# One decoder layer on one core: contiguous scratch runs, loads behind them, a shared heads bank, layer norm applied by ScalarE

## The chip, the cores and the metric

The kernel runs on 1 core of a Trainium2 chip. The metric is the device time in microseconds of one execution; a kernel's time is the median of its runs.

## The reference

Four sequences of 256 rows with 128 features pass three blocks, each with a residual and a layer norm. The context has 512 rows per sequence.

```python
x = _layernorm(x + attn(x))               # causal, 16 heads of 8, low-rank W_dq, W_uq, W_dkv, W_uk, W_uv, W_o
x = _layernorm(x + xattn(x, ctx_1024))    # keys: the 512 context rows, then x itself (causal there)
x = _layernorm(x + ffn(x))                # per feature m of 64: relu(s_m * W1 + b1) . W2, 16 inner
# in both attentions, per head:
dots = einsum(q, k) / sqrt(8); attn = softmax(dots); out = einsum(attn, v)
```

## The kernel before

**Units and steps.** A unit is one attention of one sequence: units 0 to 3 are self attention, 4 to 7 cross attention. Each has four groups of four heads, so there are 32 steps, `t` = 0 to 31, 16 of each kind. A step has three kinds of work: **S**, scores with queries on the partitions, of which VectorE takes the maximum over the keys (L1036, L869, L871); **T**, scores with keys on the partitions, whose exponential ScalarE writes into `probs` (L774); and **pv**, the product with the values (L1086). Between S and T the maxima of a step are split into three bf16 parts by GpSimd (L709 to L715), transposed (`shift`, L1097), copied by ScalarE (L801) and sent by DMA into three rows under the queries (`rows`, `send_rows`, L593), where ones under the keys meet them. So the exponential needs no bias. A self step has 4 S tiles and 4 T tiles, a cross step 12 and 12.

**Split operands.** Queries and keys are made in float32 (`qk u` for unit u, `m b` for the keys of context b) and split into three bf16 parts: ScalarE copies the high part (L789), VectorE subtracts (L886), and the middle and low parts are made by GpSimd, or by VectorE for `low_on_dve` (L601). They lie in a ring `spl` of SPL tiles. A **put** (L627) writes them to scratch in DRAM with each part as often as the products need it, six slots in all; a **take** (L646) reads them back so that 48 partitions hold six slots of eight features of one head pair. Scratch holds the features in their order, so a take has 384 runs of 1 KB per half. All puts and takes are issued by SyncE, as are the rows of cross attention; the rows of self attention go by ScalarE's queue. `ones_under` must have filled the tile before its take.

**Heads, norms and the rest.** pv adds into one half bank, `heads`; after each step ScalarE copies it to `headsT` (`drain`, L782), and the next step's pv waits for that (L1075). After four drains `norm` (L1099) transposes with eight matmuls, VectorE divides (L914, L917), and `ln1` adds x and takes moments (L899, L847); GpSimd makes `rstd` (L739, L742) and VectorE applies it (`apply`, L901). `x1T`, `qk u+4` and `v2` follow for cross attention; `yT`, `wo`, `x2T`, `s`, `hid`, `g`, `mo` after it. `v1`, `vm` and `v2` are the values.

**What sets the order.** `schedule()` (L157) plans all stages in one list with costs per engine; every engine walks that list in order, and TensorE never overtakes. `LATE` (L69) names the step before which the operands of later units are not made. Where the plan sees a gap, TensorE gets `warm` matmuls (L958). The start: DMA of `w64` and `wa`, 28 warm matmuls, six folding matmuls (L953), then qk 0, qk 1, v1 0, qk 2, v1 1. SyncE loads the context, x and the biases behind the puts of unit 0 (L643 to L645).

```python
                    if i == 0:
                        sp.dma_start(ctxT_sb[:, :], ctxT).then_inc(ctxT_in, 16)
                        sp.dma_start(x_sb[:, :, :], x_rows.rearrange("(n p) c -> p n c", p=P)).then_inc(x_in, 16)
```

## Time and profile before

| | us |
|---|---|
| Median of 3 runs | 290.76 (288.23 to 294.63) |
| The profiled execution | 293.45 |
| Its span, first to last instruction | 291.7 |
| TensorE busy | 241.0 (83%) |
| VectorE busy | 194.3 (67%) |
| ScalarE busy | 159.8 (55%) |
| GpSimd busy | 99.8 (34%) |

The profiled execution is 1.75 us longer than its span, which is time around the first and last instruction, and 2.7 us longer than the median. Durations in the profile are of this one execution. Matmuls are pipelined and their ends are modelled, so a busy TensorE is not one at its peak. "issue" as a releaser is time in which an engine waited for nothing that the profile shows; PEclk is the clock granted to TensorE, as a share of 2.4 GHz.

### The profile page before, as it was taken

How to read it: one execution, taken by the hardware profiler on the slowest of the kernel's cores; microseconds unless marked ns; L12 is line 12 of the kernel's file. 1: busy time of each engine (PE TensorE's matmuls, PEld its weight loads, DVE VectorE, ACT ScalarE, POOL GpSimd, SP SyncE). 2: the span in 40 equal slices, each digit the busy share in tenths (PEclk: the TensorE clock that was granted, in tenths of full speed). 3: DMA queues.
4: the chain of work that ended last, by engine and by line, in shares of the span. 5: the costliest groups of instructions: out<-in, count | busy, mean ns of one | idle time of the engine just before them, and what ended most of it. 6: DMA issues, size and time to landing. Idle time of an engine off the chain costs nothing.

```text
span 291.7 us, 13772 instructions
## 1 busy us (share of the span) xinstructions
PE 241.0 (83%) x5973; PEld 144.2 (49%) x5973; DVE 194.3 (67%) x429; ACT 159.8 (55%) x367; POOL 99.8 (34%) x250
## 2 busy tenths in 40 slices
PE   8920478689845699999999499999999999999882
PEld 5710336456533446756555156454654465544651
DVE  0830395785232578797999277999889997852652
ACT  1400024455523257676788255988688858879330
POOL 8650074635321142334372101522225212531131
PEclk9985595999977799999999669999999999999998
DMA  4169995101897017353639600000000000000000
GB/s 138 64 202 299 243 205 141 24 8 42 248 186 174 12 57 169 107 117 102 124 106 224 115 3 3 5 5 5 5 3 5 5 5 5 3 5 21 21 18 18
DMA packets 22716, 23.66 MB, mean 81 GB/s; under 512 B 1472, under 2 KB 20224, under 8 KB 22528
## 3 DMA queue, kind: packets, MB, share of 16 engines
q1 hardware_dynamic: 22224, 22.55, 31.7%
q8 instruction: 47, 0.77, 1.2%
q10 hardware_dynamic: 432, 0.23, 0.3%
q14 instruction: 13, 0.11, 0.1%
HBM read 12.62 MB, written 9.96 MB: 77 GB/s over the span
## 4 chain that ended last, share of the span: by engine, by line
PE 42%; DVE 19%; DMA 14%; SPq 9%; issue 7%; ACT 3%; POOL 3%; ACTq 2%; POOLq 0%; DVEq 0%
PE psum L1011 13%; PE psum L1086 10%; DVE pm L869 9%; DMA qk<-shift_rows 6%; DMA qk<-scr_qk 5%; DVE pm L871 4%; PE psum L1106 4%; PE psum L1018 3%; PE psum L958 3%; ACTq L599 2%; ACT probs L774 2%; DMA scr_m<-spl 2%; SPq L635 1%; PE psum L1173 1%; SPq L634 1%
## 5 line engine op out<-in xcount | busy, mean ns | idle before, releaser
L774 ACT ACTIVATE probs<-psum 128x512 f32<-128x512 f32 (+1 forms) x256 | 120.6, 554 | 41.6 <-PE psum L1011 20.9
L1011 PE MATMUL psum<-qk 51*32 51x128 bf16 (+3 forms) x2048 | 63.2, 266 | 31.7 <-DMA qk<-scr_qk 20.9
L871 DVE TENSOR_REDUCE pm<-psum 128x3 f32<-128x384 f32 x128 | 63.5, 550 | 36.6 <-PE psum L1018 36.5
L869 DVE TENSOR_REDUCE pm<-psum 128x1 f32<-128x512 f32 x128 | 79.1, 681 | 7.0 <-PE psum L1011 7.0
L1086 PE MATMUL psum<-probs,v 128*9 128x256 f32 (+1 forms) x1024 | 66.1, 368 | 3.5 <-issue 2.8
L1011 PEld LDWEIGHTS psum<-qk 48*32 48x32 bf16 (+1 forms) x2048 | 35.2, 96 | 56.1 <-DMA qk<-scr_qk 21.5
L1011 PE MATMUL psum<-qk,km 51*32 51x256 bf16 x1024 | 37.9, 278 | 2.8 <-DMA qk<-shift_rows 2.5
L724 POOL TENSOR_SCALAR_AFFINE_SELECT probs<-probs 128x512 f32<-128x512 f32 x32 | 20.3, 640 | 57.0 <-ACT probs L774 56.7
L1086 PEld LDWEIGHTS psum<-probs,v 128*9 128x9 f32 x1024 | 23.2, 91 | 26.0 <-issue 13.8
L1011 PE MATMUL psum<-km,qk 48*32 48x512 bf16 x512 | 35.6, 394 | 0.2
L1018 PE MATMUL psum<-neg,unit_b 64*32 64x256 bf16 x512 | 31.5, 305 | 0.0
L709 POOL CAST max_s<-maxima 128x8 bf16<-128x8 f32 x32 | 6.1, 191 | 66.4 <-DVE maxima L876 66.4
L789 ACT ACTIVATE spl<-psum 128x512 bf16<-128x512 f32 x12 | 7.2, 597 | 33.9 <-PE psum L1135 26.9
L1011 PEld LDWEIGHTS psum<-qk,km 51*32 51x32 bf16 x1024 | 15.3, 92 | 18.9 <-issue 5.5
L801 ACT ACTIVATE shift_rows<-psum 12x256 bf16<-12x256 f32 x32 | 11.5, 366 | 18.5 <-PE psum L1097 17.4
L1018 PE MATMUL psum<-negT,unit_b 64*32 64x256 bf16 x256 | 16.5, 299 | 0.0
L958 PE MATMUL psum<-warm 128*128 128x256 bf16 x97 | 15.2, 306 | 1.2 <-DVE warm L826 1.2
L1106 PEld LDWEIGHTS psum<-wa_sb,headsT 128*128 128x128 f32 x128 | 15.2, 194 | 1.7 <-DVE pm L871 0.9
L1106 PE MATMUL psum<-wa_sb,headsT 128*128 128x36 f32 x128 | 15.6, 279 | 0.1
L1011 PEld LDWEIGHTS psum<-km,qk 48*32 48x32 bf16 x512 | 12.0, 92 | 7.2 <-DVE pm L869 2.0
L1018 PEld LDWEIGHTS psum<-neg,unit_b 64*32 64x32 bf16 x512 | 14.1, 101 | 0.0
L782 ACT ACTIVATE headsT<-psum 128x256 f32<-128x256 f32 x32 | 12.0, 374 | 3.3 <-issue 2.3
(98 smaller groups left out, 263.7 us busy)
## 6 DMA issues: line engine op xcount, KB each, us to landing
qk<-scr_qk SPq DMA_DIRECT2D x16, 384.0 KB, 6.4
scr_qk<-spl SPq DMA_DIRECT2D x8, 384.0 KB, 5.1
scr_qk<-spl SPq DMA_DIRECT2D x24, 128.0 KB, 5.1
km<-scr_m SPq DMA_DIRECT2D x8, 384.0 KB, 6.8
scr_m<-spl SPq DMA_DIRECT2D x4, 384.0 KB, 3.1
ctxT_sb<-ctxT SPq DMA_DIRECT2D x1, 1024.0 KB, 5.7
scr_m<-spl SPq DMA_DIRECT2D x4, 256.0 KB, 3.5
wb_sb<-wb SPq DMA_DIRECT2D x1, 642.0 KB, 4.5
```

Source lines behind the costliest of these rows:

```text
L724: nc.gpsimd.affine_select(out=tile, in_=tile, compare_op=ALU.is_ge, fill=0.0, base=0, pattern=[[0, 2], [0, 2], [1, P]], channel_multiplier ...
L774: nc.scalar.activation(probs[:, ring % PRING, r, 0:cols], bank_of(s)[:, 0:cols], ACT.Exp, scale=SCALE).then_inc(exp_done, 1)
L782: nc.scalar.activation(headsT[:, t % (2 * NG), :], heads[:, 0:T], ACT.Copy).then_inc(drained, 1)
L789: nc.scalar.activation(parts_of(s)[0], m, ACT.Copy).then_inc(split_high, 1)
L801: last = nc.scalar.activation(shift_rows[:, t % ROWBUFS, :], m[0:PARTS * HG, 0:T], ACT.Copy, scale=-1.0)
L869: nc.vector.tensor_reduce(pm[:, place, 1 + 4 * qt:2 + 4 * qt], m, axis=AX.X, op=ALU.max).then_inc(reduced, 1)
L871: nc.vector.tensor_reduce(pm[:, place, 2:5], own_blocks(m), axis=AX.X, op=ALU.max).then_inc(reduced, 1)
L958: nc.tensor.matmul(m[:, 0:T], warm[:, 0:P], warm[:, 0:T], start=True, stop=True)
L1011: last = nc.tensor.matmul(o[STRIP * c:STRIP * (c + 1)], lhs[:, STRIP * c:STRIP * (c + 1)], rhs, start=start, stop=stop, skip_group_check=True)
L1018: last = nc.tensor.matmul(o[STRIP * c:STRIP * (c + 1)], half(unit_b, r, HALF), half(rows, r, HALF)[:, c, :, :], start=False, stop=True, sk ...
L1086: last = nc.tensor.matmul(heads[STRIP * j:STRIP * j + HS + 1, q0:T], v, weights, start=(k == 0), stop=(k == len(key_tiles(t)) - 1))
L1106: last = nc.tensor.matmul(m[:, n * cols:(n + 1) * cols], headsT[:, at, qt * P:(qt + 1) * P], used_rows, start=True, stop=True)
```

## The change

- Scratch is laid out as [half, slot, feature, ...] and the features of a half are ordered by dimension, then pair (the weights are permuted to match), so that each of the 48 partitions of a take reads one run of 8 KB. Puts and takes are made by halves of 64 partitions: 8 DMAs for a qk, 6 for an m. For qk 0 to 2 one half goes by ScalarE's queue.
- The loads of `wb`, x, biases and context stand behind the takes of units 1, 2 and 3. SPL is 5. `LATE` and the planner's costs are new. 14 warm matmuls at the start instead of 28.
- Low parts of qk 0 to 3 by VectorE. The identity casts are ScalarE's. Masks `neg` and `negT` are half as large and broadcast.
- The values have zero columns between the groups, so that groups 0 to 2 of a unit add into different rows of one half bank and group 3 into the other half; one drain of 512 columns per unit, four matmuls per norm. v2 has three buffers instead of four.
- ScalarE applies the layer norm as x * rstd + offset; GpSimd makes the offset with two more operations.

```diff
-SPL = 3
+SPL = 5
+V2BUFS = 3
 ROWBUFS = 4
-BLANK_AFTER = (2, 4, 6)
+BLANK_AFTER = (2, 4, 6, 8)
+VG, VJ = 3 * (HS + 1), 10 * (HS + 1)
+VCOLS = HG * VJ
-LATE = [(("qk", 0), 0), (("qk", 1), 0), (("v1", 0), 0), (("qk", 2), 0), (("v1", 1), 0),
-        (("m", 0), 2), (("vm", 0), 4), (("qk", 3), 6), (("m", 1), 8), (("vm", 1), 10), (("m", 2), 16), (("vm", 2), 17),
-        (("m", 3), 20), (("vm", 3), 21)]
+LATE = [(("qk", 0), 0), (("qk", 1), 0), (("qk", 2), 1), (("v1", 0), 0), (("qk", 3), 3), (("v1", 1), 2), (("m", 0), 5),
+        (("vm", 0), 11), (("m", 1), 6), (("vm", 1), 13), (("m", 2), 12), (("vm", 2), 15), (("m", 3), 22),
+        (("vm", 3), 26)]
...
-COST = {"start": 9000, "s_ahead": 3000, "t_ahead": 1300, "slack": 60, "lat": 200, "switch": 110, "load": 90,
+COST = {"start": 7500, "s_ahead": 2200, "t_ahead": 1700, "slack": 60, "lat": 200, "switch": 110, "load": 90,
...
 def low_on_dve(s):
-    return s == ("qk", 0)
+    return s[0] == "qk" and s[1] < B
+def on_both_queues(s):
+    return s[0] == "qk" and s[1] < 3
+def puts(s):
+    return 4 if s[0] == "qk" else 3
...
-        neg = sb("neg", [P, HG, 2, P], BF16)
+        neg = sb("neg", [P, HG, P], BF16)
...
-        v1 = sb("v1", [P, B * QT, NH, HS + 1])
-        v2 = sb("v2", [P, B, KT2, NH, HS + 1])
+        v1 = sb("v1", [P, B * QT, VCOLS])
+        v2 = sb("v2", [P, V2BUFS, KT2, VCOLS])
-        headsT = sb("headsT", [P, 2 * NG, T])
+        headsT = sb("headsT", [P, 2, 2, T])
...
-        scr_qk = nc.dram_tensor("scr_qk", [UNITS, P, SLOTS, 2, T], BF16, kind="Internal").ap()
-        scr_m = nc.dram_tensor("scr_m", [B, P, SLOTS, MEM], BF16, kind="Internal").ap()
+        scr_qk = nc.dram_tensor("scr_qk", [UNITS, 2, SLOTS, HALF, 2, T], BF16, kind="Internal").ap()
+        scr_m = nc.dram_tensor("scr_m", [B, 2, SLOTS, HALF, MEM], BF16, kind="Internal").ap()
...
+        def values_of(tiles):
+            heads_ = tiles.rearrange("p n (j c) -> p (n j) c", j=HG)
+            return heads_.rearrange("p n (g c) -> p n g c", c=HS + 1)[:, :, 0::3, :]
...
+        def put_half(engine, s, r):
+            what, n = s
+            i = split_no[s]
+            engine.wait_ge(split_done[i], 1)
+            parts = half(spl[:, i % SPL, :, :], r, HALF)
+            if what == "qk":
+                scr = scr_qk[n, r].rearrange("s f a t -> f s a t")
+                engine.dma_start(scr[:, 0:3, :, :], parts).then_inc(put_done[i], 16)
+                engine.dma_start(scr[:, 3:5, 0, :], parts[:, 0:4:2, :]).then_inc(put_done[i], 16)
+                engine.dma_start(scr[:, 3:5, 1, :], parts[:, 3:6:2, :]).then_inc(put_done[i], 16)
+                engine.dma_start(scr[:, 5, :, :], parts[:, 0::5, :]).then_inc(put_done[i], 16)
...
+        def take_half(engine, s, r):
+            what, n = s
+            i = split_no[s]
+            engine.wait_ge(put_done[i], put_size(i))
+            if what == "qk":
+                engine.wait_ge(qk_ones[n % B], 1)
+                src = scr_qk[n, r].rearrange("s (d p) a t -> (s d) (p a t)", p=PAIRS)
+                engine.dma_start(half(qk[:, n % B], r, DATA).rearrange("k p a t -> k (p a t)"), src).then_inc(qk_in[n], 16)
...
-            sp.dma_start(wb_sb[:, :], wb).then_inc(wb_in, 16)
-                    if i == 0:
-                        sp.dma_start(ctxT_sb[:, :], ctxT).then_inc(ctxT_in, 16)
+                    for r in range(1 if on_both_queues(s[1:]) else 2):
+                        put_half(sp, s[1:], r)
+                elif s[0] == "take":
+                    for r in range(1 if on_both_queues(s[1:]) else 2):
+                        take_half(sp, s[1:], r)
+                    if s[1:] == ("qk", 1):
+                        sp.dma_start(wb_sb[:, :], wb).then_inc(wb_in, 16)
+                    elif s[1:] == ("qk", 2):
                         sp.dma_start(x_sb[:, :, :], x_rows.rearrange("(n p) c -> p n c", p=P)).then_inc(x_in, 16)
                         sp.dma_start(bias_sb[:, :], biases.to_broadcast([P, 2 * C])).then_inc(bias_in, 16)
-                elif s[0] == "take":
-                    what, n = s[1], s[2]
-                    i = split_no[(what, n)]
-                    sp.wait_ge(put_done[i], put_size(i))
-                    if what == "qk":
-                        sp.wait_ge(qk_ones[n % B], 1)
-                        src = scr_qk[n].rearrange("(p r d) s a t -> r (d s) p (a t)", p=PAIRS, r=2)
-                        for r in range(2):
-                            dst = half(qk[:, n % B], r, DATA).rearrange("k p a t -> k p (a t)")
-                            sp.dma_start(dst, src[r]).then_inc(qk_in[n], 16)
...
+                    elif s[1:] == ("qk", 3):
+                        sp.dma_start(ctxT_sb[:, :], ctxT).then_inc(ctxT_in, 16)
...
-            nc.gpsimd.memset(v1[:, :, :, HS], 1.0).then_inc(const_v, 1)
-            nc.gpsimd.memset(v2[:, :, :, :, HS], 1.0).then_inc(const_v, 1)
-            nc.gpsimd.memset(minus_half[:, :], -0.5).then_inc(const_v, 1)
-            ones_under_memory(0)
+            nc.gpsimd.memset(v1[:, :, :], 0.0).then_inc(const_v, 1)
+            pool.wait_ge(const_v, 1)
+            nc.gpsimd.memset(values_of(v1)[:, :, :, HS], 1.0).then_inc(const_v, 1)
             ones_under(nc.gpsimd, qk[:, 3, :, 1, :]).then_inc(qk_ones[3], 1)
+            nc.gpsimd.memset(minus_half[:, :], -0.5)
+            nc.gpsimd.memset(v2[:, :, :, :], 0.0).then_inc(const_v, 1)
+            pool.wait_ge(const_v, 3)
+            nc.gpsimd.memset(values_of(v2.rearrange("p b k c -> p (b k) c"))[:, :, :, HS], 1.0).then_inc(const_v, 1)
...
+                    nc.gpsimd.tensor_scalar_mul(minus_mean[:, :], moments[:, :, 0], -1.0).then_inc(pool_step, 1)
+                    steps += 2
+                    pool.wait_ge(pool_step, steps)
+                    nc.gpsimd.tensor_tensor(rstd[:, :], vpe[:, :], minus_half[:, :], ALU.pow).then_inc(pool_step, 1)
                     steps += 1
                     pool.wait_ge(pool_step, steps)
-                    nc.gpsimd.tensor_tensor(rstd[:, :], vpe[:, :], minus_half[:, :], ALU.pow).then_inc(rstd_ready, 1)
+                    nc.gpsimd.tensor_tensor(offset[:, :], minus_mean[:, :], rstd[:, :], ALU.mult).then_inc(rstd_ready, 1)
...
+            act.wait_ge(unit_ready, 1)
+            ident = wa_sb[:, WA["ident"]:WA["ident"] + P]
+            nc.scalar.activation(ident_b[:, :], ident, ACT.Copy).then_inc(ident_ready, 1)
+            for r in range(2):
+                nc.scalar.activation(half(unit_b, r, STRIP), half(ident, r, STRIP)[:, HALF * r:HALF * r + STRIP],
+                                     ACT.Copy).then_inc(ident_ready, 1)
...
-                    act.wait_ge(pv_done, pv_no[("pv", t, len(key_tiles(t)) - 1)] + 1)
+                    act.wait_ge(pv_done, pv_no[last_pv(unit(t))] + 1)
...
-                    nc.scalar.activation(headsT[:, t % (2 * NG), :], heads[:, 0:T], ACT.Copy).then_inc(drained, 1)
+                    nc.scalar.activation(headsT[:, t // NG % 2].rearrange("p n t -> p (n t)"), heads, ACT.Copy).then_inc(drained, 1)
...
+                elif what == "apply":
+                    kind_, b = s[1], s[2]
+                    act.wait_ge(rstd_ready, ln_no[s[1:]] + 1)
+                    for i in range(QT):
+                        last = nc.scalar.activation(x1[:, b, i, :], res[:, i, :], ACT.Identity, bias=offset[:, i:i + 1],
+                                                    scale=rstd[:, i:i + 1])
+                    last.then_inc({"ln1": x1_ready, "wo": x2_ready, "mo": x3_ready}[kind_], 1)
+                elif what == "put" and on_both_queues(s[1:]):
+                    put_half(act, s[1:], 1)
+                elif what == "take" and on_both_queues(s[1:]):
+                    take_half(act, s[1:], 1)
...
-            dve.wait_ge(wa_in, 16)
-            dve.wait_ge(unit_ready, 1)
...
-                elif what == "apply":
-                    kind_, b = s[1], s[2]
-                    dve.wait_ge(rstd_ready, ln_no[s[1:]] + 1)
-                    for i in range(QT):
-                        last = nc.vector.tensor_scalar(x1[:, b, i, :], res[:, i, :], moments[:, i, 0:1], rstd[:, i:i + 1],
-                                                       ALU.subtract, ALU.mult)
-                    last.then_inc({"ln1": x1_ready, "wo": x2_ready, "mo": x3_ready}[kind_], 1)
...
-                    keep_warm(2, bank(n)[:, half_bank * T:(half_bank + 1) * T])
+                    keep_warm(1, bank(n)[:, half_bank * T:(half_bank + 1) * T])
...
-                    if k == 0 and t:
-                        pe.wait_ge(drained, t)
+                    if k == 0 and g == 0 and t:
+                        pe.wait_ge(drained, t // NG)
                     if k == 0 and g == 0:
-                        pe.wait_ge(const_v, 3)
+                        pe.wait_ge(const_v, 2 if u < B else 4)
...
-                        v = v1[:, b * QT + kt, g * HG + j, :] if u < B else v2[:, b, kt, g * HG + j, :]
+                        v = v1[:, b * QT + kt] if u < B else v2[:, b % V2BUFS, kt]
+
+                        at = VJ * j + VG * g
+                        end, at = at + HS + 1, at - (HS + 1) * (g if g < NG - 1 else 0)
+                        if k == 0 and g == 0:
+                            end = at + VG
+                        o = heads[STRIP * j:STRIP * j + end - at, (T if g == NG - 1 else 0):][:, q0:T]
                         a, r = j // 2, j % 2
                         weights = probs[:, tile_no[(t, k)] % PRING, r, a * (T - q0):(a + 1) * (T - q0)]
-                        last = nc.tensor.matmul(heads[STRIP * j:STRIP * j + HS + 1, q0:T], v, weights, start=(k == 0),
-                                                stop=(k == len(key_tiles(t)) - 1))
+                        last = nc.tensor.matmul(o, v[:, at:end], weights, start=(k == 0 and g in (0, NG - 1)),
+                                                stop=(k == len(key_tiles(t)) - 1 and g >= NG - 2), skip_group_check=True)
...
-                        pe.wait_ge(drained, ORDER.index((u, NG - 1)) + 1)
+                        at = UNIT_ORDER.index(u)
+                        pe.wait_ge(drained, at + 1)
                         for qt in range(QT):
-                            for g in range(NG):
-                                at, cols = ORDER.index((u, g)) % (2 * NG), HG * (HS + 1)
-                                n = qt * NG + g
-                                last = nc.tensor.matmul(m[:, n * cols:(n + 1) * cols], headsT[:, at, qt * P:(qt + 1) * P],
-                                                        used_rows, start=True, stop=True)
+                            for n, cols in ((0, (NG - 1) * HG * (HS + 1)), (1, HG * (HS + 1))):
+                                o = m[:, qt * NH * (HS + 1) + n * (NG - 1) * HG * (HS + 1):][:, 0:cols]
+                                last = nc.tensor.matmul(o, headsT[:, at % 2, n, qt * P:(qt + 1) * P], used_rows[n], start=True,
+                                                        stop=True)
```

## Rows read from the trace of the kernel before

**Rows 1.** The page: TensorE's line, granted clock and GB/s in 40 slices.

```profile
PE 241.0 (83%) x5973; PEld 144.2 (49%) x5973; DVE 194.3 (67%) x429; ACT 159.8 (55%) x367; POOL 99.8 (34%) x250
...
PEclk9985595999977799999999669999999999999998
...
GB/s 138 64 202 299 243 205 141 24 8 42 248 186 174 12 57 169 107 117 102 124 106 224 115 3 3 5 5 5 5 3 5 5 5 5 3 5 21 21 18 18
```

**Rows 2.** Busy time by stretch: stretch, its length, busy us (instructions) per engine.

```profile
67.00:84.00 17.00, 12.32 (x238) 8.53 (x244) 4.86 (x13) 8.25 (x20) 8.22 (x16) 1.00 0.67 163
84.00:102.00 18.00, 12.25 (x347) 7.52 (x339) 8.62 (x20) 5.38 (x13) 2.71 (x14) 0.72 0.56 115
158.00:167.00 9.00, 5.04 (x136) 2.02 (x124) 4.21 (x9) 3.61 (x8) 2.06 (x6) 0.78 0.85 144
167.00:178.00 11.00, 10.97 (x224) 6.97 (x224) 6.95 (x13) 5.29 (x12) 0.82 (x2) 0.72 0.01 2
210.00:256.00 46.00, 44.69 (x1258) 23.93 (x1254) 41.60 (x88) 36.61 (x82) 15.13 (x43) 1.00 0.02 4
...
67.00:84.00 17.00, 2.27 (x16) 1.32 (x16) 0.00 (x0) 1.00 0.67 163
```

**Rows 3.** TensorE's waits: for whom, us in total, times, longest.

```profile
PE psum L1011 <- DMA qk<-scr_qk: 20.9, 2, 16.8
PE psum L1011 <- issue: 5.8, 2, 3.2
```

**Rows 4.** Timeline of the start: start us, length us, engine, line, operation.

```profile
1.24 5.51 PE L958 MATMUL psum<-warm 128*128 128x256 bf16 x28 [1.24 <-DVE warm L826]
...
2.86 2.32 POOL L680 TENSOR_SCALAR_AFFINE_SELECT neg<-neg 32x1024 bf16<-32x1024 bf16 x2 [0.23 <-POOL negT L675]
...
7.85 0.95 POOL L591 MEMSET qk<- 128x1024 f32 x1
...
9.61 2.82 DVE L836 CAST ident_b<-wa_sb 128x128 bf16<-128x128 f32 x1
...
9.64 1.82 POOL L591 MEMSET km<- 128x2048 f32 x1
...
10.79 0.60 ACT L789 ACTIVATE spl<-psum 128x512 bf16<-128x512 f32 x1 [1.22 <-PE psum L1130]
...
14.61 0.43 DVE L609 CAST spl<-left 128x512 bf16<-128x512 f32 x1
...
15.86 0.33 SPq L633 DMA_DIRECT2D scr_qk<-spl  x1
...
23.26 1.80 SPq L655 DMA_DIRECT2D qk<-scr_qk  x2
...
33.26 0.55 PE L1011 MATMUL psum<-qk 48*32 48x128 bf16 x16 [16.81 <-DMA qk<-scr_qk]
```

**Rows 5.** Timeline and groups of the operations that change.

```profile
116.58 1.06 PE L1145 MATMUL psum<-wb_sb,ctxT_sb 128*128 128x128 f32 x8
...
270.19 1.87 PE L1106 MATMUL psum<-wa_sb,headsT 128*128 128x36 f32 x16
...
L782 ACT ACTIVATE headsT<-psum 128x256 f32<-128x256 f32 x32 | 12.0, 374 | 3.3 <-issue 2.3 <-PE psum L1086 0.8
...
L905 DVE TENSOR_SCALAR x_sb<-res,moments,rstd 128x128 f32<-128x128 f32 x24 | 7.7, 362 | 6.5 <-POOL rstd L742 6.5
...
L739 POOL TENSOR_SCALAR vpe<-moments 128x2 f32<-128x2 f32 x12 | 2.7, 223 | 29.2 <-DVE moments L852 29.2
```

**Rows 6.** DMA issues: count, KB each, median us from issue to landing.

```profile
qk<-scr_qk SPq DMA_DIRECT2D x16, 384.0 KB, 6.4
scr_qk<-spl SPq DMA_DIRECT2D x8, 384.0 KB, 5.1
...
w_sb<-w SPq DMA_DIRECT2D x1, 96.0 KB, 2.7
```

**Rows 7.** The chain that ended last, at 159 us: start, length, what.

```profile
159.26 7.69 DMA qk<-shift_rows
```

140 lines of the change are left out of this document (79 added, 61 removed).

## The prediction

> **What bounds the kernel now.** I read the page's busy shares first, then a table of stretches, then the waits of TensorE, then the timeline of the start. TensorE is busy for 83% of the span, more than any other engine, and its granted clock is 0.5 to 0.7 of full in eight of the 40 slices [rows 1]. The table of stretches says where the other 17% lie [rows 2]. Between 210 and 256 us TensorE is busy 44.69 of 46 us at full clock and VectorE 41.60: this is cross attention, and only less work helps there. Before it, three stretches are different. Nothing of attention runs before 33.3 us. From 67 to 84 us TensorE works 12.32 of 17 us, of which 2.27 are matmuls that only keep it warm, and VectorE 4.86. From 84 to 102 us it works 12.25 of 18 at 0.72 of the clock. From 158 to 167 us it works 5.04 of 9, and the eleven microseconds after that are granted 0.72. From 270 us on the tail is a chain of small steps.
>
> The waits name what is late [rows 3]: 20.9 us for takes of the first scores' queries and keys (`qk<-scr_qk`), in two waits, and 5.8 us in which nothing visible is awaited. The first of the two takes is that of unit 0 and ends at 33.26 us after a wait of 16.81 [rows 4]; the other 4.1 us end at 83.9, where unit 3 starts.
>
> **The start.** Two terms. First the order of TensorE: 28 warm matmuls last from 1.24 to 6.75 us, and the folding matmuls stand behind them, though `w64`, the first load issued, lands in 2.7 us [rows 4, 6]. With 14 of them folding can start at about 1.24 + 5.51/2 = 4.0. So the front of the chain moves up by 2.7 us, and ScalarE's high part of qk 0, ready at 11.4 before, is ready at about 8.7. VectorE, freed of the identity casts, would subtract from there and, after the 0.7 us of a subtraction, want its cast of the rest at about 9.5.
>
> Here the trace shows a hazard. The identity cast took 2.82 us from 9.61, and ended at 12.43, when GpSimd's memset of km (9.64 to 11.46) and the ones of qk behind it (0.95) were through; a cast four times as large took 0.43 us when GpSimd was idle [rows 4]. The changed GpSimd has shorter masks, then clears 2880 columns of v1 and, in one instruction, 6480 of v2. At 1.82 us for 2048 columns these are 2.6 and 5.8 us. Before, it came to the ones of qk at 7.85. Selections of half the size save 2.3 us of that (four at 1.16) and the two mask memsets, priced like the ones, 0.9; then come ones, v1 and its values, and ones again (0.95 + 2.6 + 0.3 + 0.95), so it reaches the long memset at 7.85 - 3.2 + 4.8 = 9.5 and leaves it at 15.3. I take it that the cast waits for that: 15.3 + 0.1, then two low parts of about 0.43, so that the first put is issued at 16.3, against 15.86 before. The Trainium skill (SBUF — State Buffer, the section on engine ports) says that whichever of the two starts first keeps the shared pair for its whole instruction and the other blocks. Taken literally, the outcome hangs on a tenth of a microsecond; with the cast first, the put would go at 11.5. The trace rather disagrees: a cast stamped 9.61 lost against a memset stamped 9.64. That outcome is a rival below.
>
> From the put on: before, four puts, three loads of 1.6 MB together and four puts of unit 1 came ahead of the take, which was issued at 23.26 and landed at 33.26. Now SyncE and ScalarE each issue four half puts of unit 0, then four of unit 1, then the take, and the big loads follow behind later takes.
>
> SyncE's rows before, from the first put (`scr_qk`) to the takes of units 0 and on (`qk`):
>
> ```order
> L633 DMA scr_qk<-spl 128x1536
> L634 DMA scr_qk<-spl 128x2x256
> L635 DMA scr_qk<-spl 128x2x256
> L636 DMA scr_qk<-spl 128x2x256
> L643 DMA ctxT_sb<-ctxT 128x2048
> L644 DMA x_sb<-x_rows 128x8x128
> L645 DMA bias_sb<-biases 128x256
> L633 DMA scr_qk<-spl 128x1536
> L634 DMA scr_qk<-spl 128x2x256
> L635 DMA scr_qk<-spl 128x2x256
> L636 DMA scr_qk<-spl 128x2x256
> L655 DMA qk<-scr_qk 48x8x512 x2
> ```
>
> The three loads leave this place; they stand behind the takes now. The two queues issue eight each, at some 0.5 us (15.86 to 23.26 held eleven, with the waits between): 4.2 us, to 20.5. The last put of unit 0 (issued by 18.4) needs at most the 5.1 us of [rows 6], and I take 2.7 like the small load, so 21.1; take issued by 21.6; its 0.77 MB and the 0.77 MB of unit 1's puts at some 300 GB/s (the best slice of [rows 1] is 299) plus two microseconds, hence 26. So the start gains 33.3 - 26 = 7.3 us; between 2 (takes still 9 us long) and 12 (no blocked cast).
>
> **The hole at 67 to 102 us.** The maxima of unit 3 stood first in TensorE's order and their operands were late, because qk 3 was made at step 6 and the ring of split tiles has three places. Now qk 3 is made before T0, and its take goes out with those of the first third of self attention.
>
> TensorE's rows before, where qk 3 (L1129, L1130) is made, behind T4:
>
> ```order
> L1011 MATMUL psum<-qk 32x256 x8
> L1018 MATMUL psum<-negT,unit_b 32x2x128 x4
> L1011 MATMUL psum<-qk 32x128 x8
> L1018 MATMUL psum<-negT,unit_b 32x256 x4
> L1129 MATMUL psum<-xT_sb,w 128x256
> L1130 MATMUL psum<-xT_sb,w 128x256
> L1106 MATMUL psum<-wa_sb,headsT 128x36 x8
> L1135 MATMUL psum<-ctxT_sb,wb_sb 128x512
> L1145 MATMUL psum<-wb_sb,ctxT_sb 128x128 x4
> L1097 MATMUL psum<-ident_b,max_s 12x128 x4
> ```
>
> and now (L1223, L1224), between S2 and S3:
>
> ```order
> L1098 MATMUL psum<-qk 32x128 x4
> L1098 MATMUL psum<-qk 32x256 x4
> L1105 MATMUL psum<-neg,unit_b 32x2x128 x4
> L1223 MATMUL psum<-xT_sb,w 128x256
> L1224 MATMUL psum<-xT_sb,w 128x256
> L1045 MATMUL psum<-warm 128x256 x6
> L1191 MATMUL psum<-ident_b,max_s 12x128 x2
> L1098 MATMUL psum<-qk 32x128 x4
> L1098 MATMUL psum<-qk 32x256 x4
> L1105 MATMUL psum<-neg,unit_b 32x2x128 x4
> ```
>
> The stage has moved ahead by some eight steps of scores, with nothing but latency to hide. What is lost in the two stretches: 17 - 12.32 + 2.27 = 7.0 us, 18 - 12.25 = 5.8, and 12.25 x 0.28 = 3.4 for the clock, 16.2 together [rows 2]. The 5.8 us of waits with no visible cause lie in here and may stay. I count 11; between 5 and 16.
>
> **The stretch 158 to 178 us.** Lost are 9 - 5.04 = 4.0 us and 11 x 0.28 = 3.1 by the clock. The chain has a row transfer of 7.69 us there [rows 7]: it stands behind put and take of both qk 7 and m 3 on SyncE. m 3 is now made four steps later, and each take moves 8 KB runs instead of 1 KB ones. The issue order works against it: a put is eight DMAs instead of four, so about 1.9 us more of SyncE's time ahead of the rows that follow it, on four occasions. I count a gain of 5 us (0 to 7) and a charge of 1.5 for the longer issue; the clock's share is counted in the gain.
>
> **Less work.** Norm: 16 matmul records of 1.87 us per unit now, 8 records, of which four have 108 columns: at most the 1.06 us of eight records of 128 columns [rows 5]. That saves 0.85 us x 8 = 6.8; the one or two that fall into latency-bound places give nothing, so 5.5 (4 to 7). The heads' weights are up to 27 columns wide instead of 9; the number of matmuls and their 256 moving columns stay, so I price it at nothing (up to +1). Drains: 32 of 374 ns become 8 of twice that at most, so 6 us less of ScalarE; 24 applications (362 ns each, 7.7 us together) leave VectorE and arrive at ScalarE at a like price, so ScalarE stays even. VectorE gains three low parts (1.3 us each) early. Where TensorE and VectorE are within 10% of each other, I credit 3 us (0 to 6). The scale of the layer norm becomes longer by two GpSimd operations of 0.22 us [rows 5], one of them with a hand-over: +0.45 us, and in the tail this stands on the chain three times (wo 3, mo 2, mo 3): +1.3.
>
> **The sum.** Against the profiled execution's 293.45 us (span 291.7): - 7.3 - 11 - 5 + 1.5 - 5.5 - 3 + 1.3 = -29, hence 264.4. The median of the runs shown is 290.76, 2.7 below the profiled one, so I forecast 261.7, rounded to 262. About 2% (285 to 297) is what a measurement tells from no change.
>
> **Rivals.**
> (a) All holes close. The cast is not blocked (put at 11.5, so 4.8 us more), and the hole and the row wait return 16 and 7 instead of 11 and 5: 262 - 4.8 - 7 = 250. For it: outside the named stretches TensorE is nearly full, so what is recovered there is not lost again at once; against it, the unseen waits of [rows 3] are in the hole and nothing in the change speaks of them.
> (b) A new wait takes the place of the hole at the change of kinds. qk 4 must pass x1T 0, GpSimd's low part, eight puts, six puts of m 2 (14 x 0.5 us of SyncE), and only then its take of 6.4 us: some 15 us of latency with about six steps of work in front. In this case step 16 waits as step 12 did: 4 to 8 us and a clock of 0.72 after it, so the hole returns 3 rather than 11: 271.
> (c) Slower. The take is now 48 runs of 8 KB. If the queue deals it to one or two engines instead of 16, each at 299/16 = 19 GB/s, a half of 0.384 MB lasts 20 or 10 us instead of 6.4. The start then gives back more than it gained (26 + 14 to 24), and takes 2, 4 and m 0 hold TensorE 8 to 10 us each: about 300. It decides as soon as fewer than three engines share a take. The shape 48 is the same as before, and those spread, which is against it.
> (d) Nothing, because the time is only moved: TensorE's order waits elsewhere for instructions or exps, and 286 or so remains.
>
> **How the numbers follow.** Forecast 0.52, (a) 0.20, (b) 0.18, (d) 0.06, (c) 0.04. The forecast's own terms reach from 255 to 269. With (a) and most of (b) in, the range is 248 to 279. Faster by over 2%: 0.52 + 0.20 + 0.17 = 0.89; within 2%: 0.07; slower: 0.04.
>
> **What would show it.** First scores at 26 us, with the cast of VectorE on the left tile of unit 0 ending as GpSimd's long memset does (blocked) or before 11 us (rival a). No wait for `qk<-scr_qk` over 2 us after the first; VectorE busy over 80% from 60 to 100 us. The clock at 0.9 or more between the start and the tail. Norm at 1.0 to 1.1 us on TensorE. The takes landing in 4 to 5 us instead of 6.4. I am wrong if TensorE waits 4 us or more before step 16 (b), or if takes last over 8 us (c).

## The result, and the profile after

The change made the kernel slower. The changed kernel takes 302.82 us (median of 4 runs, 302.57 to 305.72) against 290.85 us for the kernel before (median of 4, 288.23 to 294.63): a ratio of 1.047, with a 95% interval of 1.036 to 1.057. Some executions are slower whatever the kernel; medians are of all runs, ratios and intervals leave out those over 1.5% above the fastest of their kernel. The forecast was 262 us, with a range of 248 to 279. The profiled execution has a span of 300.8 us, against 291.7.

Where the 9.1 us of the two spans came in is read from four marks: the first scores, the last drain of unit 3 (end of self attention), the last drain of unit 7, and the end.

| stretch | before, us | after, us |
|---|---|---|
| start, to the first scores | 33.3 | 29.9 |
| self attention, units 0 to 3 | 94.9 | 100.6 |
| cross attention, units 4 to 7 | 141.3 | 143.5 |
| tail | 22.2 | 26.8 |

The start gained 3.4 us of the 7.3 that were forecast, and nothing behind it gained. The page of the changed kernel, with busy shares, clock, DMA share and three of the queues:

```profile
PE 246.3 (82%) x5891; PEld 143.8 (48%) x5891; DVE 194.5 (65%) x411; ACT 163.1 (54%) x370; POOL 104.9 (35%) x267
...
PEclk9955687766997687998997999999999999997987
DMA  3069546970599970256545036000000000000000
GB/s 109 0 151 212 145 108 143 224 190 3 125 190 194 218 130 3 56 117 154 108 109 110 5 70 142 7 6 3 6 5 5 4 5 3 5 20 1 20 19 20
...
q1 hardware_dynamic: 16336, 20.19, 30.4%
q10 hardware_dynamic: 2544, 2.59, 3.8%
q8 instruction: 47, 0.77, 1.1%
```

TensorE has 82 matmuls fewer than in [rows 1] and is busy 5.3 us longer: the low digits of the clock now stand in slices 3 to 10 and 13 to 16, most of self attention. All of self attention in one row, before and after:

```profile
33.30:128.20 94.90, 76.43 (x2162) 49.35 (x2166) 60.19 (x142) 44.54 (x112) 35.58 (x102) 0.89 0.52 119
```

```profile
29.90:130.50 100.60, 81.81 (x2052) 54.43 (x2060) 58.84 (x135) 43.59 (x106) 36.22 (x102) 0.80 0.61 133
```

TensorE stands idle for 18.5 us before and for 18.8 after. So of the 5.7 us that self attention lost, 5.4 are busy time, with 110 matmuls fewer and a lower clock (0.80 against 0.89), and nearly nothing is more waiting. The table of stretches (columns as in [rows 2]: busy us and count of TensorE, its weight loads, VectorE, ScalarE, GpSimd; clock; DMA share; GB/s):

```profile
29.90:66.60 36.70, 27.47 (x722) 17.37 (x726) 22.02 (x51) 10.97 (x27) 11.54 (x35) 0.73 0.70 166
66.60:96.60 30.00, 25.80 (x678) 17.63 (x680) 18.33 (x42) 14.82 (x37) 15.81 (x40) 0.84 0.57 115
96.60:116.00 19.40, 14.34 (x312) 9.73 (x292) 7.29 (x18) 8.71 (x22) 3.83 (x14) 0.76 0.75 157
130.50:170.20 39.70, 36.66 (x994) 17.76 (x984) 32.19 (x64) 27.11 (x61) 14.34 (x36) 0.91 0.50 104
204.20:237.10 32.90, 32.04 (x946) 16.73 (x934) 30.49 (x61) 25.50 (x56) 10.34 (x30) 1.00 0.02 5
```

The hole is not at 67 to 102 us any more; it is spread. Where the DMA engines are busy for 0.70 of the time, TensorE works 27.47 of 36.7 us at 0.73 of the clock; where they are at 0.02, it works 32.04 of 32.9 at full clock. The DMA share alone does not set the clock: the fastest version below has the same 0.61 over self attention and a clock of 0.88. TensorE's waits in the whole execution:

```profile
PE psum L1098 <- DMA qk<-scr_qk: 17.3, 1, 17.3
PE psum L1098 <- issue: 6.6, 3, 3.1
PE psum L1180 <- issue: 4.5, 3, 3.1
PE psum L1098 <- DMA qk<-shift_rows: 3.3, 3, 1.5
PE psum L1105 <- issue: 2.9, 1, 2.9
PE psum L1098 <- ACT shift_rows L897: 2.6, 1, 2.6
```

The second take that was late in [rows 3] (4.1 us before unit 3) is gone, as intended: one wait for `qk<-scr_qk` is left, the first. But 14.0 us are now waits in which nothing visible is awaited. Before, they were 8.6: the 5.8 of [rows 3], and these at L1086:

```profile
PE psum L1086 <- issue: 2.8, 2, 2.1
```

After the change they fall in the middle of a group of matmuls: one of 2.88 us, from 60.7 us on, stands between the scores of a tile and the mask product that belongs to them, and from 58.7 to 63.6 us the DMA share is 1.04.

The start, in order of time:

```profile
9.78 5.50 POOL L759 MEMSET v<- 128x6480 f32 x1
10.04 5.52 DVE L695 CAST spl<-left 128x512 bf16<-128x512 f32 x1
...
16.38 0.68 SPq L663 DMA_DIRECT2D scr_qk<-spl  x1
16.38 0.72 ACTq L663 DMA_DIRECT2D scr_qk<-spl  x1
...
18.21 1.16 ACTq L665 DMA_DIRECT2D scr_qk<-spl  x1
...
22.85 4.67 SPq L681 DMA_DIRECT2D qk<-scr_qk  x2
23.43 4.13 ACTq L681 DMA_DIRECT2D qk<-scr_qk  x2
...
29.86 0.55 PE L1098 MATMUL psum<-qk 48*32 48x128 bf16 x16 [17.28 <-DMA qk<-scr_qk]
```

From the memset to 16.38 us it is as predicted, nearly to the tenth: the cast of 0.43 us takes 5.52 because GpSimd's memset stands in its way, and the first put goes at 16.38. From there each put of 64 partitions holds its queue for 0.6 to 1.2 us, so the takes are issued at 22.85, and they need seven microseconds.

### The profile page after: what moved, and what is told of

It is laid out like the page before. It is cut to its first block and busy times, and to the rows that moved or that the text cites. A ratio compares the mean times of both kernels' runs of the same rounds, so it can differ in the third digit from the quotient of the medians.

```text
span 300.8 us, 13633 instructions
## 1 busy us (share of the span) xinstructions
PE 246.3 (82%) x5891; PEld 143.8 (48%) x5891; DVE 194.5 (65%) x411; ACT 163.1 (54%) x370; POOL 104.9 (35%) x267
## 5 line engine op out<-in xcount | busy, mean ns | idle before, releaser
L1098 PE MATMUL psum<-qk 48*32 48x128 bf16 (+3 forms) x2048 | 64.2, 269 | 29.9 <-DMA qk<-scr_qk 17.3
L1180 PE MATMUL psum<-probs,v 128*9 128x256 f32 (+5 forms) x1024 | 70.0, 386 | 5.0 <-issue 4.5
L1098 PEld LDWEIGHTS psum<-qk 51*32 51x32 bf16 (+1 forms) x2048 | 36.2, 97 | 53.4 <-DMA qk<-scr_qk 17.6
L1180 PEld LDWEIGHTS psum<-probs,v 128*9 128x9 f32 (+2 forms) x1024 | 25.9, 101 | 29.9 <-issue 16.0
L1098 PE MATMUL psum<-km,qk 48*32 48x512 bf16 x512 | 38.0, 395 | 0.9 <-ACT probs L859 0.2
L1098 PE MATMUL psum<-qk,km 51*32 51x256 bf16 x1024 | 33.8, 278 | 2.2 <-DMA qk<-shift_rows 1.5
L874 ACT ACTIVATE spl<-psum 128x512 bf16<-128x512 f32 x12 | 7.2, 597 | 39.7 <-PE psum L1224 27.7
L1105 PE MATMUL psum<-negT,unit_b 64*32 64x256 bf16 x256 | 16.3, 312 | 2.9 <-issue 2.9
L897 ACT ACTIVATE shift_rows<-psum 12x256 bf16<-12x256 f32 x32 | 11.4, 362 | 8.9 <-PE psum L1191 8.8
L977 DVE TENSOR_TENSOR left<-psum,spl 128x512 f32<-128x512 f32 x12 | 8.3, 692 | 12.3 <-ACT spl L874 12.2
L805 POOL TENSOR_SCALAR vpe<-moments 128x2 f32<-128x2 f32 x12 | 2.8, 230 | 35.4 <-DVE moments L943 35.2
L879 ACT ACTIVATE x_sb<-res,offset,rstd 128x128 f32<-128x128 f32 x24 | 10.7, 504 | 7.4 <-POOL offset L812 7.4
L1045 PE MATMUL psum<-warm 128*128 128x256 bf16 x79 | 12.4, 304 | 1.2 <-DVE warm L923 1.2
```

The source lines that it names most:

```text
L874: nc.scalar.activation(parts_of(s)[0], m, ACT.Copy).then_inc(split_high, 1)
L879: last = nc.scalar.activation(x1[:, b, i, :], res[:, i, :], ACT.Identity, bias=offset[:, i:i + 1], scale=rstd[:, i:i + 1])
L897: last = nc.scalar.activation(shift_rows[:, t % ROWBUFS, :], m[0:PARTS * HG, 0:T], ACT.Copy, scale=-1.0)
L977: nc.vector.tensor_sub(rest, m, high).then_inc(split_left, 1)
L1045: nc.tensor.matmul(m[:, 0:T], warm[:, 0:P], warm[:, 0:T], start=True, stop=True)
L1098: last = nc.tensor.matmul(o[STRIP * c:STRIP * (c + 1)], lhs[:, STRIP * c:STRIP * (c + 1)], rhs, start=start, stop=stop, skip_group_check=True)
```

## The experiments

Each run's ratio is to the kernel before on the same chip, with its 95% interval. The chips differ between the experiments, so ratios are compared and not times. The profiled execution is one of the runs and may lie some 2% above the median, so differences of 2 or 3 us between two profiles settle nothing alone.

### One part undone at a time

**Scratch.** `a_old_scratch` lays scratch out as before, puts whole (four transfers of 128 partitions for a qk), takes runs of 1 KB, and gives everything to SyncE; order, loads, heads bank, norms and layer norm stay changed.

```diff
-scr_qk = nc.dram_tensor("scr_qk", [UNITS, 2, SLOTS, HALF, 2, T], BF16, kind="Internal").ap()
+scr_qk = nc.dram_tensor("scr_qk", [UNITS, P, SLOTS, 2, T], BF16, kind="Internal").ap()
-for r in range(1 if on_both_queues(s[1:]) else 2):
-    put_half(sp, s[1:], r)
+put_whole(sp, s[1:])
```

> The changed kernel with the scratch of before: features in their old order, a put of 4 (qk) or 3 (m) DMAs over 128 partitions with 3 KB runs, takes of 1 KB runs, all issued by SyncE; the order of all stages is that of the changed kernel. Theory P (the new puts are what costs: runs of 1 KB or less, twice the DMAs, so the DMA engines are full for longer and the matmul engine's unseen waits rise from 8.6 to 14 us): the DMA share falls, the unseen waits fall below 9 us, unit 0 takes 32 us instead of 36.7, and the time is 288 to 295. Theory O (the new order of stages costs it): the time stays at 300 to 305. Theory Q (ScalarE's queue blocks ScalarE): 297 to 300, as in the next run.

Measured: 292.36 us, ratio 0.991 (0.981 to 1.001). The new scratch and its puts are worth 5.6 points, 16 us, the whole loss and more. Two expectations missed: unit 0 takes 36.4 us and not 32, and the waits without a visible cause rise to 17.4 us instead of falling below 9. So these waits are not the way in which the new scratch costs: the kernel that has more of them is the faster one.

**ScalarE's queue.** `a_sp_only` keeps the new scratch and the halves and issues all of them from SyncE.

```diff
-for r in range(1 if on_both_queues(s[1:]) else 2):
+for r in range(2):
```

> The changed kernel with all puts and takes of qk 0 to 2 on SyncE, none on ScalarE; nothing else moves. Theory Q (while ScalarE issues the four half puts of qk 2 it can neither copy the high part of qk 3 nor the shift rows, which costs 4 us of unit 0): first scores about 2 us later (32), but unit 0 done at 64 to 65 instead of 66.6, time 298 to 301. Theories P and O: the start's loss stays, time 303 to 306.

Measured: 309.09 us, 1.052 (1.039 to 1.066). Not faster, so ScalarE's share in the puts is not what costs in sum, though the trace of the changed kernel shows ScalarE kept from its next high part for 6.0 us by six issues between 37.0 and 43.0, and TensorE waiting 2.6 us for the shift rows behind them. At the start the second queue does help: without it the first scores come at 34.3 us instead of 29.9. Of the whole, nothing can be told apart (1.052 against 1.047).

**Layer norm by VectorE again**, without GpSimd's two operations for the offset:

```diff
-last = nc.scalar.activation(x1[:, b, i, :], res[:, i, :], ACT.Identity, bias=offset[:, i:i + 1], scale=rstd[:, i:i + 1])
+last = nc.vector.tensor_scalar(x1[:, b, i, :], res[:, i, :], moments[:, i, 0:1], rstd[:, i:i + 1], ALU.subtract, ALU.mult)
```

> The changed kernel with the layer norm applied by VectorE as before, and without the two GpSimd operations for the offset. Three applications stand on the chain of the tail; each should be 0.45 us (GpSimd) and 0.3 us (0.60 instead of 0.88 for two halves) shorter. If that is all the tail lost: tail (from the last drain) 26.8 becomes 24.5, time 299 to 301. If ScalarE's in-order wait for the offset also costs in units 5 to 7: 296 to 299.

Measured: 301.21 us, 1.031 (1.021 to 1.041), 1.6 points better than the change, with intervals that overlap. The tail says it more clearly: it shrinks from 26.8 to 23.0 us, and over all profiles here it is 25.4 to 27.4 us in the seven versions in which ScalarE applies, and 23.0 or 23.1 in the seven with the new order in which VectorE does (26.5 in the one with the old table).

**The memset of v2 later**, behind the low part of qk 1:

```diff
+            pool.wait_ge(split_done[1], 1)
             nc.gpsimd.memset(v2[:, :, :, :], 0.0).then_inc(const_v, 1)
```

> The changed kernel with GpSimd's memset of 6480 columns held back until the low part of qk 1 is done. If VectorE's cast is 5.5 us long only because of that memset: the cast takes 0.43 us, the first put goes at 11.3 instead of 16.4, first scores at 25 instead of 29.9. If what follows is bound by these: time 297 to 299. If later waits (ring, DMA) take it back: 301 to 303.

Measured: 303.69 us, 1.034 (1.021 to 1.046). First scores at 25.6 us instead of 29.9, so the blocked cast cost 4.3 us there; but the ratio moved by 1.3 points (3.8 us) with overlapping intervals. Whether the start's gain lasts to the end is not shown.

### What about the scratch costs

**Halves in the old layout**: the number of transfers without the short runs. Against the run with the old scratch:

```diff
-            parts = spl[:, i % SPL, :, :]
+            parts = half(spl[:, i % SPL, :, :], r, HALF)
             if what == "qk":
-                scr = scr_qk[n]
+                scr = half(scr_qk[n], r, HALF)
...
-                    put_whole(sp, s[1:])
+                    for r in range(2):
+                        put_half(sp, s[1:], r)
```

> The changed kernel with scratch laid out as before (puts in runs of up to 3 KB), everything on SyncE, but each put still made by halves of 64 partitions: 8 transfers for a qk, 6 for an m. It stands between two kernels already measured: the new layout on SyncE alone (309.1 us) and the old layout with whole puts (292.4 us), which differ by 16.7 us. Theory N, the number of transfers (each issue about 0.6 us of SyncE): near 309, at least 304. Theory R, the short runs of a put in the new layout (1 KB and 512 B instead of 3 KB): near 292, at most 296.

Measured: 305.84 us, 1.045 (1.024 to 1.065). Theory N holds: with the old layout and old runs, putting by halves alone costs 5.4 of the 5.6 points. Halving is two things at once, twice the transfers and 64 partitions in each; they are taken apart below. Against the new layout on the same queue (1.052) nothing is left that can be told apart.

**Whole puts in a new layout** (scratch as [slot, feature], so that whole puts can be written):

```diff
-src = scr_qk[n, r].rearrange("s (d p) a t -> (s d) (p a t)", p=PAIRS)
+src = scr_qk[n, :, HALF * r:HALF * r + HALF].rearrange("s (d p) a t -> s d (p a t)", p=PAIRS)
```

> The changed kernel with the new order of the features and takes of 8 KB runs, everything on SyncE, but each put made whole (4 transfers of 128 partitions for a qk, 3 for an m); scratch is [slot, feature] so that this can be written. Theory N (number of transfers): near 292, at most 296. Theory R (1 KB runs of the puts): near 309, at least 304. If both share it, 298 to 303.

Measured: 311.81 us, 1.064 (1.045 to 1.082). Neither theory: the edit brought something of its own. The source of a take is now 6 rows of 8 runs instead of 48 runs. The stretches from first put to take and from take to first scores, first of the old layout with whole puts:

```profile
16.40:20.80 4.40, 0.06 (x1) 0.00 (x0) 1.73 (x4) 0.00 (x0) 0.00 (x0) 0.97 0.79 274
20.80:28.10 7.30, 0.01 (x4) 0.01 (x4) 0.00 (x0) 0.00 (x0) 0.00 (x0) 0.50 1.03 209
```

then of halves in the old layout:

```profile
16.40:26.80 10.40, 0.00 (x0) 0.00 (x0) 1.75 (x4) 0.00 (x0) 0.00 (x0) 0.50 0.61 140
26.80:34.20 7.40, 0.03 (x4) 0.03 (x8) 0.00 (x0) 0.00 (x0) 0.00 (x0) 0.50 0.96 168
```

and of whole puts in the new layout:

```profile
16.40:21.20 4.80, 0.02 (x1) 0.00 (x0) 1.74 (x4) 0.00 (x0) 0.00 (x0) 0.92 0.80 256
21.20:33.40 12.20, 0.03 (x4) 0.03 (x8) 0.00 (x0) 0.00 (x0) 0.00 (x0) 0.50 0.65 146
```

The whole puts go out in 4.8 us, as they should, but the takes need 12.2 us at a DMA share of 0.65, where 48 runs of 8 KB (7.4 us with the new scratch on SyncE alone) and 384 runs of 1 KB (7.3 us) both fill the engines. The Trainium skill (DMA: Bandwidth & Descriptors, the section on why a DMA increments its semaphore by 16) says that the engines are dealt by the outermost dimension of both sides, the largest number up to 16 that divides them; for 6 and 48 that is 6. The share of 0.65 agrees in direction, since the load of `wb` lies in the same stretch; which engines carried the take, no trace here shows. If the rule is at work, it is the mechanism of rival (c), which the changed kernel itself does not have.

The halves' row shows the price: 10.4 us for the same bytes, at 140 GB/s. The Trainium skill (SBUF — State Buffer, the section on the DMA port swizzle and the one on issuing two DMAs to hit both halves) has a rule that I had not weighed: 64 neighbouring partitions reach half of the ports, and two such transfers do not add up to a whole one. Whether bytes or issues cost was tried in the changed kernel itself. In nine of the twelve puts (all but those of qk 0, qk 4 and m 0) each transfer moves 16 of its 64 partitions, and the takes read the scratch of the first unit of their kind, so the other units compute with the wrong operands:

```diff
+            if n and s != ("qk", B):
+                scr_ = slice(0, 16)
+            else:
+                scr_ = slice(None)
+            parts = parts[scr_]
...
-src = scr_qk[n, r].rearrange("s (d p) a t -> (s d) (p a t)", p=PAIRS)
+src = scr_qk[origin, r].rearrange("s (d p) a t -> (s d) (p a t)", p=PAIRS)
```

> The changed kernel itself (302.8 us) with the same taken away: the transfers of all puts but those of qk 0, qk 4 and m 0 move 16 of their 64 partitions, and takes read the first unit of their kind. All the issues of the halves stay, on both queues. Theory: the halves cost by the DMA engines' time (140 GB/s at a busy share of 0.6 against 274 GB/s at 0.8 for whole puts): then 290 us or less. Rival: they cost by the time of the issues on SyncE and ScalarE, which stays: 298 us or more. Between them both have a share.

Measured: 301.46 us, 1.032 (1.001 to 1.063). Three quarters of the bytes of nine puts are gone, and the time stays within the interval of the change. The issues became shorter too: SyncE is held for 0.30 to 0.58 us by one of 16 partitions, where it was 0.58 to 0.61. This speaks for the number of transfers and against their bytes, and with them against the port rule, though its direction shows in 140 against 274 GB/s. It does not settle it: the interval holds the change's own ratio and reaches down to 1.001. The same cut in the version with whole puts, below, ran on the same chip and took 0.959. Of the 7.3 points between the two, 2.9 are what layer norm and memset gave singly, so some 4 points are left to the halves with few bytes in either.

### The three undone together

`b_combined` has whole puts in the old scratch, layer norm by VectorE and the late memset.

> The changed kernel with three parts undone together: scratch layout and whole puts as before (0.991 of the kernel before when alone), layer norm applied by VectorE (it gave 1.5% alone), and the long memset of v2 moved behind the low part of qk 1 (1.3% alone). If the three add: 0.991 - 0.015 - 0.013 = 0.963, some 283 us, faster than both kernels. If the latter two only gave what the crowded start hid: 0.985 or so.

Measured: 284.69 us, 0.971 (0.958 to 0.985): faster than both kernels, but by a point less than if the three gains added up. What is left of the change there is the order, the loads behind, the short norms, the shared bank, the smaller masks and the shorter warm-up.

**Two queues for whole puts** of units 0 and 1:

```diff
+                elif what == "put" and s[1:] in EARLY:
+                    put_whole(act, s[1:], (2, 3))
+                elif what == "take" and s[1:] in EARLY:
+                    take_half(act, s[1:], 1)
```

> The version with three parts undone, with whole puts of 128 partitions, but for units 0 and 1 two of the four transfers of a put and one of the two takes go by ScalarE's queue. It asks whether the second queue was the good part of the change and only the halves the bad one. Expected: takes issued at 13.5 to 14 instead of 15.8 us, first scores at 21 instead of 22.8, time 1 to 2 us less (283). Rival: the DMA engines are the limit (they were busy 79% in the stretch of whole puts), so nothing: within 0.5 us.

Measured: 286.46 us, 0.984 (0.974 to 0.994), not faster than one queue. From first put to first scores it took 10.6 us against 11.4, so the second queue gains 0.8 us at most. The first put itself was later, at 13.9 instead of 11.4 us, for a reason told in the last section.

### The order

**The old table with everything else of the combined version**: the due steps and the planner's weights of before.

```diff
-LATE = [(("qk", 0), 0), (("qk", 1), 0), (("qk", 2), 1), (("v1", 0), 0), (("qk", 3), 3), (("v1", 1), 2), (("m", 0), 5),
+LATE = [(("qk", 0), 0), (("qk", 1), 0), (("v1", 0), 0), (("qk", 2), 0), (("v1", 1), 0),
...
-COST = {"start": 7500, "s_ahead": 2200, "t_ahead": 1700, "slack": 60, "lat": 200, "switch": 110, "load": 90,
+COST = {"start": 9000, "s_ahead": 3000, "t_ahead": 1300, "slack": 60, "lat": 200, "switch": 110, "load": 90,
...
```

> As the run with three parts undone, and also with the order of before: its table of due steps and its planner weights (qk 3 at step 6, m 0 at step 2, m 3 at step 20), while the ring of five split tiles, the loads behind takes, the shared heads bank and the short norms stay. Theory O, the new order is what gains (it closed the wait before unit 3): 6 to 12 us slower than the run with three parts undone, with a wait for qk<-scr_qk over 3 us near unit 3. Rival, the new order costs as much as it gains, since unit 7 took 4 us longer and the tail 4: within 3 us of that run or faster.

Measured: 301.00 us, 1.026 (1.010 to 1.042), 5.5 points slower. The expected wait for `qk<-scr_qk` did not come back (only the first is there, 14.5 us), but the first unit of cross attention took 49.5 us instead of 37.7. The run does not have the order of the kernel before, though. The planner of the changed kernel lets nothing that needs the context go ahead of the take of unit 3, behind which the context is loaded, and the old table makes qk 3 at step 6. So the keys of context 0 are made at 90.4 us, with those of context 1 at 93.4, where the kernel before made the first at 35.6. First this run, then the kernel before:

```profile
90.36 1.02 PE L1220 MATMUL psum<-ctxT_sb,wb_sb 128*128 128x512 f32 x2
```

```profile
35.62 1.62 PE L1135 MATMUL psum<-ctxT_sb,wb_sb 128*128 128x512 f32 x2
```

What is shown is that the old table does not fit the new place of the context's load; what the old order itself would cost there is not shown.

**The new table alone**, in the kernel before, with five split tiles and the loads behind the take of unit 1 (the lines of the diff above with their signs turned round, and these):

```diff
-SPL = 3
+SPL = 5
...
+                    if (what, n) == ("qk", 1):
+                        sp.dma_start(ctxT_sb[:, :], ctxT).then_inc(ctxT_in, 16)
```

> The kernel before with the order alone changed: the new table of due steps and planner weights, a ring of five split tiles, and the three loads behind the take of unit 1. No other part of the change. Theory O: the order is the part that gains (with the other parts in place the old order cost 16 us), so 8 to 12 us faster than the kernel before, 282 to 286, and the second wait for qk<-scr_qk (4.1 us at 84 us) is gone. Rival: order and the other parts only gain together, then within 4 us of before.

Measured: 309.44 us, 1.059 (1.040 to 1.079). Both theories fall: the new table and weights lose 17 us here. At the end of unit 3 it is 1.0 us ahead; unit 4 then takes 49.3 us against 42.8, with a row transfer of 6.3 us that TensorE waits for, and unit 7 takes 40.1 us against 32.4. This run too has an order of its own: the planner of the kernel before does not know that it must wait for the context, and makes the keys of context 0 at 41.1 us, where the changed kernel makes them at 70.8. So the same table gives different orders in the two kernels, and neither run says what the changed kernel's order is worth by itself. The planner's costs describe a kernel with the other parts; which of them the table needs was not tried.

**The loads alone**, in the kernel before:

```diff
-                    if i == 0:
-                        sp.dma_start(ctxT_sb[:, :], ctxT).then_inc(ctxT_in, 16)
...
                             sp.dma_start(half(km[:, n], r, DATA), src[r]).then_inc(m_in[n], 16)
+                    if (what, n) == ("qk", 1):
+                        sp.dma_start(ctxT_sb[:, :], ctxT).then_inc(ctxT_in, 16)
...
```

> The kernel before with nothing changed but the place of the three loads (context, x, biases): behind the take of unit 1 instead of behind the put of unit 0. The take of unit 0 then is issued about 1.5 us earlier and shares the DMA engines with no 1.6 MB of loads: it should land in 7.3 us instead of 10, so first scores at 29 to 30 instead of 33.3 us. Theory: 3 to 4 us faster, 290 or so. Rival: what the start gains is lost at the first stage that needs the context (due at step 2): within 1 us.

Measured: 297.11 us against 295.05 on the same chip, and 291.53 against 290.12 for the fastest runs: no difference is shown. First scores at 27.1 us, 6.2 earlier, more than expected; last drain of unit 3 at 128.4, where it was. The waits show the payment, since the first product with the context, due at step 2, now waits for its load:

```profile
PE psum L1011 <- DMA qk<-scr_qk: 14.7, 2, 11.1
PE psum L1135 <- DMA ctxT_sb<-ctxT: 6.2, 1, 6.2
```

### Where the start's gain goes

**More transfers where there are none.** To the combined version, copies of 1.5 MB from scratch to scratch were added in cross attention:

```diff
 send_rows(sp, s[1])
+if 21 <= s[1] < 28:
+    sp.dma_start(dump[s[1] - 21], scr_qk[0:2]).then_inc(dumped, 16)
```

> The version with three parts undone, plus work that computes nothing: behind the rows of steps 21 to 27, in cross attention, SyncE copies 1.5 MB from the scratch of units 0 and 1 to another scratch. TensorE's program is the same. In this stretch (about 180 to 240 us) the DMA engines are otherwise idle and TensorE has no wait without a visible cause. Theory F: those waits come from DMA engines that are full (the transfers that bring instructions are late): waits named issue of 1 to 3 us each now show between 180 and 240 us, 5 us or more together, with a lower clock behind them, and the time rises by 5 to 15 us. Rival: they have nothing to do with transfers: none over 0.5 us there, and the time rises only by waits for rows.

Measured: 301.20 us, 1.036 (1.021 to 1.050), 16.5 us or 6.4 points more than without. Waits of TensorE from 165 to 250 us:

```profile
PE psum L1095 <- issue: 7.2, 3, 3.4
PE psum L1177 <- issue: 4.3, 2, 3.6
PE psum L1095 <- DVE pm L952: 0.2, 1, 0.2
```

and two of the stretches there:

```profile
229.00:234.90 5.90, 2.50 (x83) 0.90 (x71) 3.40 (x7) 2.50 (x5) 0.79 (x4) 0.96 0.35 136
235.00:240.00 5.00, 5.00 (x95) 2.27 (x87) 2.83 (x5) 3.59 (x8) 1.23 (x2) 0.50 0.02 5
```

The combined version has no such wait over 0.5 us behind 150 us. Here are 11.5 us in five waits, all behind the issue of the first copy at 161.9, and there is none for a row transfer. Over cross attention TensorE stands idle 10.4 us longer than in the combined version, and is busy 7.3 us longer: the second row shows how, since after the wait of 3.4 us TensorE is busy all the time and at half clock. So copies do hold TensorE up, in waits that no releaser explains. It is not that all DMA engines are busy just then. In three of the five waits their share is 0.03 or less, and what these three have in common is the end: TensorE goes on at 195.39, 207.70 and 234.86 us, and a copy had landed at 195.2, 207.5 and 234.6. What TensorE awaits there the profile does not show. That a transfer of the `instruction` queue (47 in all) stands behind the copy is likely, but argued, not shown.

**Fewer bytes where there are many**: the combined version with the puts of 16 partitions, as above.

> The version with three parts undone (284.7 us), with the bytes of the puts taken away: every put but those of qk 0, qk 4 and m 0 still issues its four or three transfers, each of 16 partitions instead of 128, to scratch that nobody reads, and the takes of the other units read the scratch of unit 0, unit 4 or context 0 instead of their own. So TensorE's program, the waits and the number of transfers stay; 9 of the 12 puts lose seven eighths of their bytes. The attention results of the other units are not those of the reference. Theory F, that full DMA engines hold up TensorE through late instructions and then its clock: self attention (first scores to last drain of unit 3, 94.5 us) shortens by 5 us or more, its waits without visible cause fall from 13 to 8 us or less, and the time is 276 to 280. Rival: the stretch is bound by the chain of each step, and stays within 2 us.

Measured: 278.22 us, 0.959 (0.944 to 0.974); self attention 93.6 us against 94.6, and 16.0 us of waits without visible cause, no fewer. The ratio fell by 1.2 points with intervals that overlap, and the stretch did not shorten. Undecided for the puts. The waits stand elsewhere: one of 4.55 us up to 49.0 us, with the DMA share at 1.15, where x and the context are loaded behind takes.

**The loads back at the start**, in the combined version:

```diff
                     put_whole(sp, s[1:])
+                    if s[1:] == ("qk", 0):
+                        sp.dma_start(ctxT_sb[:, :], ctxT).then_inc(ctxT_in, 16)
...
```

> The version with three parts undone (284.7 us; first scores at 22.8 us, self attention 94.5 us from there), with one more edit: the context, x and the biases are loaded behind the put of unit 0, as in the kernel before, instead of behind the takes of units 2 and 3. Theory G, the loads that move out of the start are paid back in self attention (full DMA engines at 44 to 57 us, two waits of TensorE without visible cause of 3.1 and 3.9 us there, and the lower clock behind them): first scores 4 to 6 us later, self attention shorter by as much, those two waits gone, and the time within 2 us. Rival: the later loads are free, so the start's loss stays: 289 us or more.

Measured: 284.79 us, 0.977 (0.965 to 0.988), the same time as without. From 44 to 60 us, combined version first, this one second:

```profile
44.00:60.00 16.00, 9.07 (x222) 5.06 (x216) 5.15 (x12) 4.68 (x12) 3.75 (x12) 0.71 0.74 166
```

```profile
44.00:60.00 16.00, 14.37 (x490) 9.29 (x476) 10.99 (x27) 6.23 (x16) 7.39 (x22) 0.71 0.64 146
```

First scores 6.4 us later (29.2), last drain of unit 3 at 117.7 instead of 117.4: nearly all of it regained, and the two waits of 3.1 and 3.9 us in this stretch are gone. Theory G holds for the time. It does not hold for the waits as a whole, which sum to 14.2 us against 14.9. Of the 6.1 us by which self attention is shorter, 4.1 are busy time at a higher clock (0.88 against 0.84) and 2.0 are idle time.

**The loads right behind the take of unit 1**:

```diff
 if s[1:] == ("qk", 1):
     sp.dma_start(wb_sb[:, :], wb).then_inc(wb_in, 16)
+    sp.dma_start(ctxT_sb[:, :], ctxT).then_inc(ctxT_in, 16)
+    sp.dma_start(x_sb[:, :, :], x_rows.rearrange("(n p) c -> p n c", p=P)).then_inc(x_in, 16)
+    sp.dma_start(bias_sb[:, :], biases.to_broadcast([P, 2 * C])).then_inc(bias_in, 16)
-elif s[1:] == ("qk", 2):
...
-elif s[1:] == ("qk", 3):
...
```

> The same version with the three loads behind the take of unit 1, so that they fall on the time in which TensorE waits for the first take and on the first steps, and delay no take. By theory G this has the early start (first scores at 23 to 24 us) and not the full engines at 44 to 57 us: 2 to 5 us faster, 280 to 282. Rival: as in the kernel before with the same edit (6 us gained at the start, all given back): within 2 us of 284.7.

Measured: 279.55 us, 0.959 (0.945 to 0.973), the fastest kernel whose work is whole: 4.1% less than before, 8.8 points less than the change. On the same chip it lies 5.2 us under the version with the loads at put 0, and no run of one reaches into those of the other (277.49 to 281.58 against 284.06 to 285.27). First scores at 25.6 us, last drain of unit 3 at 115.5. Its waits without visible cause are still there, 13.3 us in all, but none is over 2.5 us:

```profile
PE psum L1088 <- issue: 5.2, 6, 1.7
PE psum L1170 <- issue: 3.5, 4, 1.6
PE psum L1181 <- issue: 2.5, 1, 2.5
PE psum L1095 <- issue: 2.1, 3, 1.2
```

The marks of the versions side by side, all from profiled executions:

| kernel | first scores | self attention | TensorE busy in it | its clock | unseen waits | end of unit 7 | span |
|---|---|---|---|---|---|---|---|
| before | 33.3 | 94.9 | 76.4 | 0.89 | 8.6 | 269.5 | 291.7 |
| changed | 29.9 | 100.6 | 81.8 | 0.80 | 14.0 | 274.0 | 300.8 |
| old scratch, whole puts | 28.1 | 94.3 | 76.5 | 0.84 | 17.4 | 267.4 | 294.8 |
| halves, old layout, SyncE | 34.2 | 102.2 | 84.2 | 0.77 | 15.7 | 278.3 | 303.7 |
| changed, puts of few bytes | 29.3 | 99.9 | 80.6 | 0.80 | 19.6 | 275.1 | 300.5 |
| three undone | 22.8 | 94.6 | 78.1 | 0.84 | 14.9 | 256.6 | 279.7 |
| three undone, loads at put 0 | 29.2 | 88.5 | 74.0 | 0.88 | 14.2 | 259.9 | 283.0 |
| three undone, loads at take 1 | 25.6 | 89.9 | 75.1 | 0.88 | 13.3 | 256.6 | 279.6 |

"Unseen waits" are TensorE's waits over the whole execution in which the profile shows nothing awaited. They do not follow the time. Among the versions of the changed kernel, the clock in self attention does.

## Why the prediction was wrong

Two terms carry the miss. The longer issue of the puts was priced at 1.5 us and costs some 16, and the hole was to return 11 us and returned none. The others are smaller, and most of them missed in the same direction.

**The start, -7.3 forecast, -3.4 measured.** The reading of the hazard was right: reached 9.5 forecast, 9.78 measured; left 15.3, and 15.28; put at 16.3, and 16.38. Some luck is in it. The front of the chain came forward by 2.1 us and not by 2.7, because 14 warm matmuls took 3.17 us and not half of 5.51, and the first folding product behind them 0.94 us instead of 0.71; so the cast was stamped 10.04, clearly behind the memset, and the tie of a tenth did not arise. Of the 3.9 us that are missing, 1.3 are the issue of the puts, "at some 0.5 us": sixteen puts on two queues took 6.5 us, not 4.2. The stretch that the prediction cites held eleven in 7.4 us, which is 0.67 each, and these were transfers of 128 partitions; of 64, one holds its queue for 0.6 us where only one queue issues and for up to 1.2 where two do. The other 2.6 us are the takes, 7.0 us and not 4.4, and here the sum itself is wrong: its 1.54 MB at 300 GB/s and its two microseconds are 7.1 us, and would have given 28.7 and not 26. That this comes so near the 7.0 measured is luck again, since the stretch moved 213 GB/s and not 300.

**The extra issues, +1.5 forecast.** This is the step that turned the sign: undone by itself, the kernel is not slower than before. "About 1.9 us more of SyncE's time ahead of the rows that follow it, on four occasions" was priced at 1.5. Undoing it and nothing more (halves to whole, old layout, one queue) is worth 5.4 points, 16 us or so. Eight issues of 0.65 us, the gap included, are 5.2 us per put against 2.0 for four of 0.33 to 0.53: 3.2 us, not 1.9, and the put stands in the chain put, take, scores of each of the twelve operands, where I had counted four. In the traces the halves are 14 us behind at the end of unit 3, 6.1 of them at the start and 7.9 in self attention. First whole puts, then halves, both in the old layout:

```profile
28.10:122.40 94.30, 76.52 (x2052) 50.54 (x2060) 59.35 (x135) 43.75 (x107) 36.03 (x102) 0.84 0.58 142
```

```profile
34.20:136.40 102.20, 84.20 (x2052) 56.14 (x2060) 60.30 (x135) 43.65 (x106) 36.28 (x102) 0.77 0.63 131
```

TensorE stands idle for 17.8 us in the first and 18.0 in the second. The 7.9 us are the same 2052 matmuls at a lower clock, although the first execution lay 5.7 us above its median. Why putting by halves lowers the clock is open; the waits without a releaser do not explain it, since they are 17.4 us with whole puts and 15.7 with halves.

**The hole, -11 forecast.** The wait for unit 3's take went, as said. What it should have returned did not come. The term counted on idle time that closes and on a clock that rises with it; TensorE's idle time in self attention stayed (18.5 us before, 18.8 after), its clock fell from 0.89 to 0.80, and self attention took 5.7 us longer. Two causes are shown. One is the halves. The other is that the loads were moved out of idle time into work: the same 1.6 MB that delayed a start in which TensorE had nothing to do now are issued from 53 us on (TensorE works 10.09 of the 16 us from 50 to 66, with the DMA engines busy 0.90 of the time) and take TensorE's time and clock; the kernel before gains 6.2 us at the start by moving them and has lost it at the end of unit 3, and the combined version loses 6.4 by moving them back and has regained all but 0.4 there. I had written that the unseen waits "may stay". In self attention they doubled, from 6.5 to 13.5 us, and took up the idle time that the named waits gave back. They stood in [rows 2] beside DMA shares of 0.67 and 0.56, and that a change which moves transfers under TensorE's work moves them too was the sentence to price. They are no measure of the loss by themselves: the kernel with the old scratch has more of them and is through self attention in 94.3 us. Rival (d), the time only moved, had 0.06, and named instructions; it was the nearest to what happened, and its price of 286 had neither the halves nor the tail.

**158 to 178 us, -5 forecast.** The 4.0 us lost up to 167 were read as the row transfer of [rows 7]. TensorE's own waits there are 2.1 us without a releaser and 1.9 for rows. After the change the first is 0.5 and the second 1.5, and unit 4 gained 3.1 us (39.7 against 42.8), given back in unit 7 (36.9 against 32.4). m 3 is due two steps later in the new table (22 against 20), not four. Rival (b), TensorE waiting for the take of qk 4 before step 16, did not come in the changed kernel; its own 8 us would have made 270 and not 271. Where the new table stood alone, TensorE waited 6.3 us in unit 4, but for rows.

**Less work, -8.5 forecast.** The norms cost 1.08 us, as said (a saving of 0.8 us each, 6.3 and not 6.8), and the wider weights nothing: the median pv matmul is 379 ns in both kernels between 172 and 230 us, at a clock of 0.99 and 1.00. But cross attention took 2.2 us longer, so no gain can be shown for norms, drains or applications. The credit of 3 us for less VectorE and ScalarE work was wrong by the profile's own word: TensorE was busy 97% there.

**ScalarE's application, "at a like price", +1.3 forecast.** The tail grew by 4.6 us, and 3.8 of them go when VectorE applies. Three rows of the tail:

```profile
288.32 0.20 POOL L812 TENSOR_TENSOR offset<-minus_mean,rstd 128x2 f32<-128x2 f32 x1
289.11 0.60 ACT L899 ACTIVATE ctxT_sb<-psum 128x512 f32<-128x512 f32 x1 [2.62 <-PE psum L1259]
...
289.60 0.87 ACT L879 ACTIVATE x_sb<-res,offset,rstd 128x128 f32<-128x128 f32 x2
```

An application takes 504 ns (362 on VectorE, [rows 5]), and on ScalarE it stands behind the copy L899, which waits for TensorE: the offset is there at 288.5, and the application begins at 289.6. With a clock of 0.88 instead of 0.94 in the tail, 1.3 became 4.

**Rival (c)** had the wrong size for the changed kernel (takes landed in 6.0 us, against 6.4 in [rows 6] and 6.3 with the old scratch and the new order, so 8 KB runs are hardly faster than 1 KB runs) and, by the rule cited above, the right mechanism for the run with six outer rows.

Of the signs, the blocked cast came and no later take was waited for. VectorE was busy 53% of the time from 60 to 100 us and not 80%, and the takes did not land in 4 to 5 us.

## What to carry to other kernels

Count a transfer's issue on its queue by its own shape, and multiply by every hand-over in the chain: two transfers of 64 partitions are not one of 128. A load that delays an idle start is not expensive; moved under TensorE's work it can cost all that it gave, so place it where TensorE is waiting anyway. Split a stretch into idle time and busy time before you explain it: here the waits changed their names and kept their sum, and the loss was in the clock. And a planner's table is not an order: the same table gave other orders in a kernel with other parts, and lost 6% there.

## What the runs showed that I had not expected

- Copies that TensorE's program has nothing to do with cost it 16.5 us: 11.5 us are waits without a releaser, three of which end within 0.3 us of the landing of a copy while the DMA share is 0.03 or less, and the work behind the last of them runs at half clock.
- A take of the same bytes and the same run length of 8 KB needs 12.2 us with 6 outer rows and 7.4 with 48.
- The start runs at either of two speeds. In six of the fifteen profiles with 14 warm matmuls qk 0's two matmuls took 1.22 us instead of 0.70, and where GpSimd's memset does not hide it, the first put goes 2.5 us later. The granted clock in that stretch reads 1.00 at both speeds. First of the run with three parts undone, then of that with the loads at take 1:

```profile
7.60 0.70 PE L1215 MATMUL psum<-xT_sb,w 128*128 128x256 f32 x2 [0.37 <-ACT w L843]
```

```profile
9.20 1.22 PE L1213 MATMUL psum<-xT_sb,w 128*128 128x256 f32 x2 [0.37 <-ACT w L841]
```

The rows show where the two part: behind the warm matmuls every profile begins folding at the slower speed, nine reach the faster one by 6.1 us, and the other six are still at the slower one at 12 us. In the three profiles with 28 warm matmuls it was not seen; whether more of them would fix it was not tried.
